# Rotating the columns before the query and key products instead of the products after them

## The reference

```python
q = (x @ Wq.T).reshape(b, t, NH, D)          # NH = 32 heads, D = 4
k = (x @ Wk.T).reshape(b, t, NH, D)
v = (x @ Wv.T).reshape(b, t, NH, D)
# rope: halves u1, u2 of a head; cos, sin of t * inv_freq, two frequencies
q, k = [concatenate([u1 * cos - u2 * sin, u1 * sin + u2 * cos]) for (u1, u2) in (q, k)]
phi_q, phi_k = elu(q) + 1, elu(k) + 1
beta = clip(sigmoid(x @ Wbeta.T + bbeta), BMIN, BMAX)      # M = 2 decays a head
mix = softmax(x @ Wmix.T + bmix)
# scan over t:  K = K * beta + phi_k;  S = S * beta + phi_k (x) v
# y = sum over m of (phi_q . S) / (phi_q . K + EPS) * mix
y = ys @ Wout.T + bout;  out = layer_norm(x + y) * ln_g + ln_b
```

## Time and profile before

| | |
|---|---|
| median of 3 runs | 1453.92 us (1448.1 to 1456.07) |
| the profiled execution's own time | 1457.73 us |
| its span, first to last instruction | 1454.8 us |
| PE, DVE, ACT, POOL busy | 80%, 78%, 73%, 18% of the span |
| TensorE's granted clock, mean | 0.899 |

### The profile page before, as it was taken

One profiled execution on the slowest core, in us unless ns is written; L12 is line 12 of the kernel. 1 busy time (PEld: TensorE's weight loads), 2 busy tenths in 40 slices (PEclk: granted clock), 3 DMA queues, 4 the chain that ended last, 5 costly groups with the idle time before them and its releaser, 6 DMA issues.

```text
span 1454.8 us, 18749 instructions
## 1 busy us (share of the span) xinstructions
PE 1157.6 (80%) x5194; PEld 706.2 (49%) x5194; DVE 1134.4 (78%) x1637; ACT 1059.1 (73%) x2849; POOL 264.5 (18%) x382
## 2 busy tenths in 40 slices
PE   5375878989797888889897988889897979878653
PEld 3133444645455554646454555546464555546332
DVE  6758595969798897969797988969797979864613
ACT  4153857779696969777796969687877969677553
POOL 1001121021212111130213122211303121211000
PEclk9676988989899999989899989999899989989776
DMA  4000000010101010100101010101001010101010
GB/s 127 0 8 8 8 15 8 9 29 1 30 8 30 8 30 9 30 7 7 29 0 30 7 29 7 30 7 22 15 7 26 4 29 8 22 8 23 0 22 15
DMA packets 28360, 25.84 MB, mean 18 GB/s; under 512 B 2304, under 2 KB 21376, under 8 KB 28288
## 3 DMA queue, kind: packets, MB, share of 16 engines
q0 software_dynamic: 6912, 12.59, 5.0%
q1 hardware_dynamic: 12928, 8.29, 1.9%
q10 hardware_dynamic: 8448, 4.20, 0.9%
HBM read 8.28 MB, written 4.19 MB: 9 GB/s over the span
## 4 chain that ended last, share of the span: by engine, by line
DVE 26%; PE 23%; issue 22%; ACT 20%; POOL 6%; DMA 2%; ACTq 1%; SPq 0%; DVEq 0%; POOLq 0%
PE ps L923 4%; PE ps L1236 3%; DVE hid L1440 3%; ACT hq L525 2%; PE ps L1125 2%; DVE hid L1663 2%; DVE blk L1427 2%; DVE outer L1582 2%; DVE state L1591 2%; PE ps L1202 2%; PE ps L996 2%; DVE hid L1441 2%; ACT norm L515 2%; POOL rstd_of_f L425 2%; DVE hid L1433 2%
## 5 line engine op out<-in xcount | busy, mean ns | idle before, releaser
L1125 PE MATMUL ps<-wguT,hqcol 128*128 128x352 f32 x512 | 179.8, 483 | 17.7 <-ACT th L708 7.4
L1591 DVE TENSOR_TENSOR_SCAN state<-beta,outer 128x512 f32<-128x512 f32 x128 | 148.3, 1199 | 0.0
L1125 PEld LDWEIGHTS ps<-wguT,hqcol 128*128 128x128 f32 x512 | 93.8, 197 | 86.1 <-issue 25.1
L1440 DVE SCALAR_TENSOR_TENSOR hid<-hidcol,hid 128x1408 f32<-128x1408 f32 (+1 forms) x68 | 106.4, 1569 | 11.3 <-ACT hidcol L717 10.7
L923 PE MATMUL ps<-const,hq 128*128 128x128 f32 x128 | 37.8, 386 | 88.5 <-ACT hq L515 88.4
L1427 DVE TENSOR_REDUCE xblk<-ps 128x32 f32<-128x512 f32 x32 | 22.0, 687 | 100.2 <-PE ps L1063 100.2
L1236 PE MATMUL ps<-hidcol,wdT 128*128 128x256 f32 (+1 forms) x384 | 92.6, 392 | 0.0
L1663 DVE TENSOR_TENSOR hid<-th,ps 128x352 f32<-128x352 f32 x128 | 63.1, 514 | 25.6 <-PE ps L1125 17.3
L1236 PEld LDWEIGHTS ps<-hidcol,wdT 128*128 128x128 f32 (+1 forms) x384 | 73.8, 196 | 18.7 <-issue 6.7
L996 PE MATMUL ps<-state,const 128*32 128x512 f32 x256 | 74.0, 884 | 7.2 <-DVE state L1617 7.1
L1617 DVE TENSOR_TENSOR state<-state,rope 128x1024 f32<-128x1024 f32 x64 | 75.0, 1213 | 1.7
(11 more groups left out here) (242 smaller groups left out, 3331.8 us busy)
## 6 DMA issues: line engine op xcount, KB each, us to landing
xa<-in_x SPq DMA_DIRECT2D x16, 256.0 KB, 2.9
xa<-zn POOLq DMA_DIRECT2D x16, 256.0 KB, 3.3
xb<-arow POOLq DMA_DIRECT2D x16, 256.0 KB, 3.3
xb<-drow POOLq DMA_DIRECT2D x16, 256.0 KB, 3.3
out<-xb ACTq DMA_DIRECT2D x16, 256.0 KB, 2.3
const<-in_const SPq DMA_DIRECT2D x1, 848.0 KB, 7.1
state<-in_wmod SPq DMA_DIRECT2D x1, 768.0 KB, 4.8
wqk<-in_wqk SPq DMA_DIRECT2D x1, 256.0 KB, 4.5
```

The source lines that it names most:

```text
L1125: t_.matmul(bank(f"f{l}_{'gu'[g]}{t}")[:, 0:I_FF], hqcol[l][:, t * P:(t + 1) * P], wguT[:, l, g, :], start=True, stop=True).then_inc(s_gu[ ...
L1440: return v.scalar_tensor_tensor(dst, mag, low, dst, ALU.max, (ALU.add, ALU.subtract)[part])
L1591: return v.tensor_tensor_scan(state[:, m, c, :], beta[:, m, :], src, 0.0, ALU.mult, ALU.add)
```

## The change

The rotation is moved ahead of the products. Since cos and sin depend only on the token and on one of two frequencies, `a2x` on DVE multiplies the normalized columns `hcol[0]` by four tables (cos and sin of the two frequencies, the same in every partition) into `rope`, 128 x 4 x 256 values for each sequence of the pair. PE then multiplies them by the plain and by the swapped matrix, whose columns are sorted by frequency (64 and 64) and carry the sign, and sums the two in PSUM: eight products with 64 columns of weights for a pair in place of four with 128, each into one half of the partitions. The rotated key and query come out in one bank each; `a2r` is gone, and ACT's `a2` and DVE's `a2p` read the bank. `eqk` and `qshare` become tiles of their own. The order of the partitions of heads changes accordingly in the selection matrices, in `wv_rep`, `wb_rep` and `bbeta`; DVE sorts `wqk` once before the first pair.

The residuals are still added by POOL's DMAs. The bank of every product, all `freed` waits and the order of all four engines' bodies are written anew. The bodies are cut at another place: what was turn n of stage `a` is now spread over n (`a1s` part 0) and n-1.

```diff
+        eqk = sb("eqk", [P, 2, TOK])
+        qshare = sb("qshare", [P, M, TOK])
             def a2(i, h):                                    # PE
-                after(pe, s_hcol[0], i, SEQ)
+                after(pe, s_turned, i, SEQ)
...
+                dst = bank(("a_fk", "a_fq")[h])
                 for n_, k in enumerate(((2, 3), (0, 1))[h]):
-                    ins = t_.matmul(two_banks(("a_k", "a_q")[h])[:, n_, :], wqk[:, k, :], hcol[0][:, :], start=True, stop=True)
+                    for f in range(2):
+                        ins = t_.matmul(dst[f * 64:(f + 1) * 64, :], wqk[:, k, f, :], rope[:, 2 * f + n_, :], start=(n_ == 0), stop=(n_ == 1))
                 ins.then_inc(s_qk_mm, 1)
...
-            def a2(i, h):                                    # DVE
-                k = 1 - h
-                after(dve, s_qk_mm, i, 2, h + 1)
-                v.tensor_tensor(rope[:, 2 * k:2 * k + 2, :], two_banks(("a_k", "a_q")[h]), tab, ALU.mult).then_inc(s_rope_mul, 1)
-
-            def a2r(i, h):
-                k = 1 - h
-                after(dve, s_rope_mul, i, 2, h + 1)
-                v.tensor_tensor(qk[:, k, :], rope[:, 2 * k, :], rope[:, 2 * k + 1, :], ALU.add).then_inc(s_roped, 1)
+            def a2x(i, q):
+                after(dve, s_hcol[0], i, SEQ, q + 1)
+                before(dve, s_qk_mm, i, 2)
+                toks = slice(q * T, (q + 1) * T)
+                v.tensor_tensor(rope[:, :, toks], hcol[0][:, toks].unsqueeze(1).to_broadcast([P, 4, T]), tab, ALU.mult).then_inc(s_turned, 1)
...
             def a2p(i, h):
-                v.scalar_tensor_tensor(phi[:, k, :], qk[:, k, :], 0.0, eqk[:, k, :], ALU.max, ALU.add).then_inc(s_phi, 1)
+                v.scalar_tensor_tensor(phi[:, k, :], bank(("a_fk", "a_fq")[h]), 0.0, eqk[:, k, :], ALU.max, ALU.add).then_inc(s_phi, 1)
...
             def a2(i, n_):                                   # ACT
-                s.activation(eqk[:, k, :], qk[:, k, :], ACT.Relu, scale=-1.0).then_inc(s_nexp, 1)
+                s.activation(eqk[:, k, :], bank(("a_fk", "a_fq")[n_]), ACT.Relu, scale=-1.0).then_inc(s_nexp, 1)
```

More of the change, by code:

```diff
@@ L198, in build @@
         qk = sb("qk", [P, 2, TOK])
-        eqk = rope[:, 0:4:2, :]
+        eqk = sb("eqk", [P, 2, TOK])
         phi = qk
         outer = sb("outer", [P, D, TOK])
+        wqk_raw = outer[:, 0, :].rearrange("p (k n) -> p k n", k=4)
         beta = sb("beta", [P, M, TOK])
@@ L205, in build @@
         share = sb("share", [P, T])
-        qshare = rope[:, 2:4, :]
+        qshare = sb("qshare", [P, M, TOK])
         ycol = sb("ycol", [P, TOK])
@@ L789, in body @@
             def body(n):
+                do(c2n, n - 3)
+                do(a6s, n - 2)
+                do(c2, n - 3)
+                do(a1n, n - 1)
+                do(a6n, n - 2)
+                do(a1, n - 1, 0)
+                do(a7, n - 2, 0)
+                do(a7, n - 2, 1)
+                do(a1, n - 1, 1)
+                do(c4, n - 3, 0)
+                do(a8, n - 2)
+                do(c4, n - 3, 1)
+                s.preload_act_table_set("natural_log_exp_and_others")
+                do(c4e, n - 3, 0)
@@ new lines, in body @@
+                at_start(weight_blocks, n - 1, 0, 0, 6)
+                do(c4a, n - 3, 0)
+                do(c4a, n - 3, 1)
+                do(a2x, n - 1, 0)
+                at_start(weight_blocks, n - 1, 0, 0, 7)
+                do(layer(b1q, 1), n - 4, 1)
+                do(mean_f0, n - 2)
+                do(layer(b1q, 1), n - 4, 2)
+                do(c4b, n - 3)
+                do(a2x, n - 1, 1)
+                at_start(weight_blocks, n - 1, 0, 0, 8)
+                do(c4s, n - 3, 0)
@@ L1860, in body @@
[L1860 to L1868 removed]
+                do(a1s, n, 0)
             turns(dve, body)
```

731 lines of the change are left out of this document (351 added, 380 removed), and 10 rows, old and new, of the table BANK.

## The result

The changed kernel takes 1445.59 us (median of 10 runs, 1442.29 to 1447.4), the kernel before 1455.49 in the same comparison: ratio 0.9939, 95% interval 0.9924 to 0.9953. It is faster, by 9.9 us (0.6%); the forecast was a gain of 24 to 25. The profiled execution has a span of 1445.0.

A forecast was written before the change was run, and what follows sets the result against it. No engine is full; a turn is a chain passing between nearly full engines, VectorE's work binding only its last part. 14 x 2.0 = 28 less, 2.7 more in setup gave 1432.4, 1428.6 by the median, said as 1430; range 1400 to 1458.

The forecast's parts named there:

- VectorE's work, PSUM in place of SBUF, the products: Rotation: some 22 us less VectorE work in all; reading PSUM costs nothing; 1.72 us per query or key product, as before.
- The setup: Before the first pair: eight small VectorE operations, six more copies and one more DMA add 2.7 us, bounds 1 and 4.
- strict program order: Rival, chance 0.09: on TensorE, half-wide products hold each other back, 0.86 us more a turn, 12 us in all: 1442.
- C, 42.9: Turn from c4b to b4q's end, VectorE nearly gapless: 42.8 less 0.7, but two new waits, giving 42.9 us.
- B, 7.4: Turn from c4a to c4b, a chain past the second exponential: 7.4 us against 8.2 before.
- A, 27.8: Turn from b4q's end to c4a, a chain over several engines: 27.8 us, 1.3 sooner; 27.1 at high clock, 29.3 at low.
- 14 x 2.0 = 28: Whole run: 14 turns, each shortened by 2.0 us (78.1 against 80.1), take 28 us off.
- The turn of 80.1 as a baseline: One whole loop turn of the kernel before, b4q's end to b4q's end, 80.1 us, from which the gain was reckoned.
- the gap eats the gain: Rival, chance 0.14: b4q's end to c4a takes 29.3 us or more, turn 79.6 to 80.1: 1450 to 1456.
- The low clock goes away: Rival, chance 0.14: TensorE's idle before b1T_1 shrinks, clock stays at 1.00, 3.6 us less a turn: 1407.
- the rival on it: Rival, chance 0.05: filling and draining 5% longer, 16 us, with the turn at 80 as before: near 1470.

The follow-up runs named there:

- wo_warm_adds: Changed kernel with all bodies written out, three unread products of constants on TensorE, and two 128x512 additions put back on VectorE each turn: 1421.04 us, ratio 0.9767.

## Why the forecast was half right

- *VectorE's work, PSUM in place of SBUF, the products*: right. The removed work is 21.0 us for 22, and the rest is within 0.1 us an operation. The setup took 1.7 for 2.7. The halves run side by side; the rival of strict program order would have shown as 0.43 us more in each group of eight, and the group takes 0.06 more. The Trainium skill (TensorE: Matmul & The Clock Gate, section "The mechanism" of Part 3) says that matmuls start and end in program order; the measurement doesn't bear it out for these eight, and decides.
- *C, 42.9*: 42.9 in the loop, where it was 42.9 before as well. The walk's own reason held: the removed addition becomes the wait for b1R_0 (0.62 after, 0.65 said). Put back, it fills that wait. So the work taken off VectorE was worth nothing by itself, in B or in C (wo_warm_adds, written out and at 1.00).
- *B, 7.4*: right in sign, 7.0 measured.
- *A, 27.8*: this is the first step that failed. Measured: 28.7 in the mean of the turns without a way back, 30.5 with one. With the clock at 1.00 and without loops A is 27.85, where I had 27.1, and the kernel before has 27.74 there: the new order didn't shorten A at all. Missing from the walk are the 1.0 us that VectorE waits for `mixp` and the 1.0 us by which b5_0 and b5d_0 end later than the 5.0 "as before", since b6c_1 and c8 stand in front of them on ScalarE; the last a4m ends at 20.0 and not 18.9. Each was taken away alone or with the other, and A didn't get shorter, so what they cost together is argued only.
- *14 x 2.0 = 28*: this is the second. One turn was walked and multiplied; "the bodies are cut at another place" stood in the change, and no price was put on it. The way back of the loop is four times in the span, it costs 2.1 us bare and 2.4 with the clock that falls after it, and the new cuts put it in the gap of A. 4 x 2.4 = 10 us. With cuts at covered places 7 of these came back.
- *The turn of 80.1 as a baseline*: it contained 1.3 us that go with the loop and its cut, or a long low stretch. Written out, the kernel before gains 14 us by itself, more than the 9 of the changed one. So the way back explains why the new turn came out longer than it was walked, but not why the change is worth little: without loops it is worth 2.5 to 5 us, since A doesn't gain and the low stretch costs the new order 1.25 us a turn.
- *The sum*: a turn without a way back kept 1.6 of 2.0, and there the errors cancel in part, 0.9 too little in A and 0.4 too much in B. The ways back took 10 us, and the time up to the first c4b 2.3. From first to last c4b 1202.2 became 1190.2: 12.0 us less, and 12.0 - 2.3 = 9.7 of span.
- *Rivals*: by its number "strict program order" (1442) came nearest, by luck, since its mechanism isn't there. By its reason it was "the gap eats the gain" (1450 to 1456), A near its upper bound. "The low clock goes away" did not happen by itself; made to happen, it is worth 1436.4 - 1421.0 = 15 us written out (18 by the ratios).
- *Slips that changed nothing*: draining is 245 us where the rival on it says 249, and the key and the query each hold one PSUM bank less, not two.
